# Moving the weight stream from the scalar engine's DMA queue to the sync engine's, with new orders for blocks 1 to 7

## What is computed

```python
xn = _layernorm(x)
x = x + attn(xn) + ffn(xn)

# attn: chunked linear attention with decay, 16 heads of 32, chunks of 128 tokens
h = _rmsnorm(xn, qkv_norm_w); q, k, v = h @ ternary(qkv_w).T
scores = einsum('bhtd,bhsd,hts->bhts', qi, ki, mask)
intra  = einsum('bhts,bhsd->bhtd', scores, vi)
cross  = einsum('bhtd,ht,bhde->bhte', qi, lam_t, S)
S      = lam_T * S + einsum('bhtd,ht,bhte->bhde', ki, lam_rev, vi)
out = _rmsnorm(_rmsnorm(intra + cross, norm_w), proj_norm_w) @ ternary(proj_w).T

# ffn: 512 -> 2048 -> 512
gated = silu(xn @ w_gate.T) * (xn @ w_up.T)
y = gated @ w_down.T
```

## Time and profile before

| | |
|---|---|
| median of 3 runs | 1535.77 us (1535.44 to 1554.81) |
| profiled execution, whole | 1534.2 us |
| its span, first to last instruction | 1532.4 us |
| TensorE busy (PE) | 1339.8 us, 87% |
| its weight loads (PEld, beside PE) | 903.7 us, 59% |
| VectorE busy (DVE) | 1088.7 us, 71% |
| ScalarE busy (ACT) | 648.5 us, 42% |
| GpSimd busy (POOL) | 294.3 us, 19% |
| queue q1 (SP) | 125.09 MB, 35.2% of the 16 engines' span |
| queue q10 (ScalarE) | 88.10 MB, 18.5% |
| mean granted TensorE clock | 0.959 of full |

### The profile page before, as it was taken

One profiled execution on the slowest core, in us unless ns is written; L12 is line 12 of the kernel. 1 busy time (PEld: TensorE's weight loads), 2 busy tenths in 40 slices (PEclk: granted clock), 3 DMA queues, 4 the chain that ended last, 5 costly groups with the idle time before them and its releaser, 6 DMA issues.

```text
span 1532.4 us, 26734 instructions
## 1 busy us (share of the span) xinstructions
PE 1339.8 (87%) x10060; PEld 903.7 (59%) x10060; DVE 1088.7 (71%) x2118; ACT 648.5 (42%) x1275; POOL 294.3 (19%) x296
## 2 busy tenths in 40 slices
PE   5899999988689988889987899888987889878899
PEld 3465545543376664666756676576755767557675
DVE  6989966977556786567865689476893658946576
ACT  7955424655233352334524335243442433424342
POOL 5400001455111211112111122011220112201111
PEclk9999999999889999999999999899998999989999
DMA  7232342477955349553594435944468543595342
GB/s 295 93 101 90 77 124 87 161 232 233 220 139 132 121 128 167 138 141 111 146 181 127 136 107 146 199 131 108 128 162 160 140 91 127 148 163 147 87 132 54
DMA packets 242558, 214.89 MB, mean 140 GB/s; under 512 B 147456, under 2 KB 212992, under 8 KB 240768
## 3 DMA queue, kind: packets, MB, share of 16 engines
q1 hardware_dynamic: 228320, 125.09, 35.2%
q10 hardware_dynamic: 14112, 88.10, 18.5%
HBM read 130.82 MB, written 23.07 MB: 100 GB/s over the span
## 4 chain that ended last, share of the span: by engine, by line
PE 55%; DVE 18%; issue 9%; DMA 8%; SPq 5%; ACT 3%; POOL 2%; ACTq 0%; DVEq 0%; POOLq 0%
PE bank L679 30%; PE bank L811 22%; DMA k_stack<-k_parts 4%; SPq L1234 3%; DVE stage L995 2%; DMA q_stack<-q_parts 2%; PE bank L721 2%; DVE arena L1109 2%; DVE wide L1661 1%; DMA wide<-up_t 1%; SPq L1335 1%; DVE sm_lo L995 1%; DVE xin L1132 1%; DVE sm L1037 1%; SPq L1236 1%
## 5 line engine op out<-in xcount | busy, mean ns | idle before, releaser
L811 PE MATMUL bank<-wide 128*128 128x256 f16 x4032 | 498.2, 281 | 38.3 <-issue 38.1
L811 PEld LDWEIGHTS bank<-wide 128*128 128x128 f16 x4032 | 402.8, 101 | 100.6 <-issue 40.9
L679 PE MATMUL bank<-wd_hi,arena 128*128 128x512 f16 x1024 | 326.3, 385 | 17.1 <-DVE arena L1109 14.5
L1204 POOL TENSOR_TENSOR wide<-wide 128x512 f32<-128x512 f32 x96 | 125.9, 1314 | 823.8 <-ACT wide L958 823.8
L679 PE MATMUL bank<-wd_lo,arena 128*128 128x512 f16 x512 | 197.1, 385 | 0.0
L679 PE MATMUL bank<-xt,wide 128*128 128x512 f16 x768 | 178.1, 387 | 6.7 <-ACT sg L972 3.3
L679 PEld LDWEIGHTS bank<-wd_hi,arena 128*128 128x128 f16 x1024 | 101.4, 99 | 138.3 <-DVE arena L1109 18.8
L1109 DVE SCALAR_TENSOR_TENSOR arena<-bank,small,arena 128x512 f32<-128x512 f32 x160 | 119.4, 746 | 41.3 <-PE bank L679 31.1
L1037 DVE TENSOR_TENSOR sm<-bank,mask 128x512 f32<-128x512 f32 x128 | 87.6, 684 | 71.9 <-PE bank L721 71.6
L679 PE MATMUL bank<-ht,wq 128*128 128x256 f16 x1024 | 127.6, 274 | 7.2 <-DVE arena L1109 3.5
L872 ACT ACTIVATE sm_hi<-sm 128x512 f16<-128x512 f32 x128 | 80.0, 625 | 127.0 <-DVE sm L1037 126.9
(11 more groups left out here) (215 smaller groups left out, 1928.4 us busy)
## 6 DMA issues: line engine op xcount, KB each, us to landing
wide<-made ACTq DMA_DIRECT2D x96, 896.0 KB, 5.6
made<-wide SPq DMA_DIRECT2D x16, 896.0 KB, 5.4
k_stack<-k_parts SPq DMA_DIRECT2D x192, 64.0 KB, 2.2
q_stack<-q_parts SPq DMA_DIRECT2D x192, 64.0 KB, 2.3
arena<-x SPq DMA_DIRECT2D x8, 1024.0 KB, 5.9
out<-arena SPq DMA_DIRECT2D x32, 256.0 KB, 10.4
xin<-x SPq DMA_DIRECT2D x30, 256.0 KB, 4.7
stage<-up_t SPq DMA_DIRECT2D x4, 1024.0 KB, 5.4
```

The source lines that it names most:

```text
L679: last = e.matmul(dst, a, b, start=start and n == 0, stop=stop and n == len(lhs) - 1)
L811: last = e.matmul(dst, tile_weights(h, n // 2, w, k), tile_x(n % 2, b, k), start=start and (k, n) == (0, 0), stop=(k, n) == (1, 2), skip_g ...
L1204: e.tensor_tensor(up[h % 2], up[h % 2], gt[h % 3], ALU.mult).then_inc(po["GT"].sem, 1)
```

## The change

ScalarE's list loses item `LW` (16 a steady block, 4 in block 1). SP's list gets the same items, with the same waits and the same transfer: the stream now runs in q1, first in, first out with the fills of the stacks, the loads, the stores and the transposes. The lists of blocks 1 to 7 are written anew on all engines; each holds the same items as before. In block 1 the two transposes of `xs` become an item `MC` of their own. Block 0's lists are as before.

```diff
-    return it[0] in ("ST", "XN", "TX", "TT", "XC", "TH", "XT") or it[0] == "LW" and it[1] >= HT
+    return it[0] in ("ST", "XN", "TX", "TT", "XC", "TH", "XT", "MC") or it[0] == "LW" and it[1] >= HT
...
-        elif kind == "LW":
-            h = it[1]
-            if is_plain(blk):
-                e.wait_ge(st_b[BUILD_SLOT[h - HT]], 16 * turn(h - HT))
-                e.wait_ge(pe["U"].sem, pe["U"].at(blk, 12 if h < HT + 2 else HT))
-            else:
-                e.wait_ge(pe["P3"].sem, pe["P3"].at(blk, h - RING + 1))
-            e.dma_start(ring[h % RING], made[h % HT, :, :]).then_inc(ld_w[h % RING].sem, 16)
...
-                    elif kind == "LW" and is_plain(blk) and n == HT + 2:
+                    elif kind == "LW":
+                        if is_plain(blk):
+                            e.wait_ge(st_b[BUILD_SLOT[n - HT]], 16 * turn(n - HT))
+                            e.wait_ge(pe["U"].sem, pe["U"].at(blk, 12 if n < HT + 2 else HT))
+                        else:
+                            e.wait_ge(pe["P3"].sem, pe["P3"].at(blk, n - RING + 1))
+                        e.dma_start(ring[n % RING], made[n % HT, :, :]).then_inc(ld_w[n % RING].sem, 16)
+                    elif kind == "MC":
                         for m in range(2):
                             e.wait_ge(st_b[m], 16 * BUILD_SLOT.count(m))
                         for p in range(2):
```

Of the steady list of SP, two lines:

```diff
-        ('K', 0), ('Q', 0), ('V', 0), ('KT', 0), ('K', 1), ('Q', 1), ('KT', 1), ('K', 2), ('Q', 2), ('KT', 2), ('K', 3),
+        ('K', 0), ('Q', 0), ('V', 0), ('KT', 0), ('LW', 4), ('Q', 1), ('K', 1), ('KT', 1), ('LW', 5), ('LW', 6), ('LW', 7),
```

More of the change, by code:

```diff
@@ L166 @@
     "PE": [
[3 rows of a table removed]
[3 rows of a table added]
         ('SC', 2, 0), ('U', 3), ('KV', 2), ('O', 2, 0), ('SC', 2, 1), ('Q', 3), ('K', 3), ('G', 4), ('U', 4), ('OX', 2, 0),
[10 rows of a table removed]
[10 rows of a table added]
     ],
     "ACT": [
[14 rows of a table removed]
[14 rows of a table added]
     ],
     "DVE": [
[18 rows of a table removed]
[18 rows of a table added]
     ],
     "POOL": [
-        ('BA', 0), ('BA', 1), ('NR', 0), ('BA', 2), ('BA', 3), ('ST', 0), ('BA', 4), ('BA', 5), ('BA', 6), ('BA', 7),
-        ('BA', 8), ('BA', 9), ('TT', 0), ('BA', 10), ('BA', 11), ('BA', 12), ('BA', 13), ('NR', 1), ('BA', 14), ('BA', 15),
+        ('BA', 0), ('BA', 1), ('NR', 0), ('BA', 2), ('ST', 0), ('BA', 3), ('BA', 4), ('BA', 5), ('BA', 6), ('BA', 7),
+        ('TT', 0), ('BA', 8), ('BA', 9), ('BA', 10), ('BA', 11), ('BA', 12), ('BA', 13), ('NR', 1), ('BA', 14), ('BA', 15),
         ('ST', 1), ('TT', 1),
@@ L234 @@
     "PE": [
[17 rows of a table removed]
[18 rows of a table added]
     ],
     "ACT": [
[17 rows of a table removed]
[15 rows of a table added]
     ],
     "DVE": [
[20 rows of a table removed]
[19 rows of a table added]
     ],
     "POOL": [
-        ('UG', 0), ('UG', 1), ('UG', 2), ('UG', 3), ('UG', 4), ('UG', 5), ('UG', 6), ('UG', 7), ('UG', 8), ('NR', 0),
-        ('ST', 0), ('UG', 9), ('UG', 10), ('TT', 0), ('UG', 11), ('UG', 12), ('UG', 13), ('UG', 14), ('UG', 15), ('NR', 1),
+        ('UG', 0), ('UG', 1), ('UG', 2), ('UG', 3), ('UG', 4), ('UG', 5), ('UG', 6), ('UG', 7), ('NR', 0), ('UG', 8),
+        ('UG', 9), ('UG', 10), ('ST', 0), ('TT', 0), ('UG', 11), ('UG', 12), ('UG', 13), ('UG', 14), ('UG', 15), ('NR', 1),
         ('ST', 1), ('TT', 1),
```

## The result

The changed kernel takes 1383.74 us (median, 1378.71 to 1388.07) against 1543.55 for the kernel before in the same comparison: ratio 0.896, 95% interval 0.888 to 0.904. That is 160 us, more than twice the 73 that were forecast, and 41 us under the low end of the range. Measured once more on another chip the ratio was 0.895 (0.891 to 0.899).

What follows compares the result with a forecast made beforehand. TensorE sets the pace, with 144 us idle in blocks 2 to 7, mostly behind DMAs, and clock 0.95. 39 + 0 + 8 + 40 + 12 - 26 = 73 us off 1534.2 gives 1461, median 1463; range 1425 to 1522.

Steps and rivals of the forecast that it cites:

- waits before `SC`: TensorE waiting for stack fills: 28 us saved at `SC 1 0`, 12 at other steps, 26 charged for the shared queue.
- what the queue adds: Fills behind loads in q1 at steps 2, 4, 5, 6, 7: 26 us lost, about 2 at two places a block.
- starts of blocks 3 to 7: Waits before the first tile work for the second `xs` transpose go whole: 30.0 us.
- passage to block 2: Block 1 to 2: VectorE's later chain and a clean transpose cancel, 0; bounds 5 gained, 10 lost.
- slow matmuls: Matmuls slowed after long waits speed up: 9 us at block starts, 12 after `SC 1 0`.
- Block starts: First tile work, steady blocks: clean second `xs` transpose saves 30 us of waits and 9 of slow matmuls; bounds 30 and 39.
- `KV 0` and `SC 1 0`: Early products and `SC` whose transfers have loads beside them: 8 us and 40 us saved, the latter including slow matmuls.
- The other stack waits: Waits for `k_stack` and `q_stack` fills: a quarter of 47.7 us, 12, saved; bounds 0 and 30.
- the block starts alone: Rival, chance 0.18: only block starts gain, queue losses eat `SC`, `KV` and stack gains; 1497 us.
- Block 1: Block 1 and its passage to block 2: 0 taken; bounds 5 us gained, 10 lost.
- All of it: Rival, chance 0.12: new lists land every fill in time, 130 us less 20 for meeting VectorE; 1426 us.
- the signs named for the forecast: Second `xs` transpose 6 to 9 us, `SC 1 0` wait under 2 us, clock over 0.96, idle near 85 us.

Runs made afterwards that it cites:

- The two loads alone: `LW 18` and `LW 19` moved ahead in ScalarE's list, right behind `TD 15`, queue unchanged, against the kernel before: 1494.81 us, ratio 0.969.
- Alone 41: `LW 4` to `LW 7` of blocks 2 to 7 moved from ScalarE's list to SP's, against the kernel before: 1501.63 us, ratio 0.974.
- the ten loads in question: `LW 8` to `LW 17` of blocks 2 to 7 moved from ScalarE's list to SP's, against the kernel before: 1497.56 us, ratio 0.983.

## Why the prediction was wrong

The direction, the places and the loads as the cause held; the size did not, by a factor of 2.2. The step that failed is the account of the waits before `SC`: 28 and 12 us saved, less 26 for what the queue adds. In the two profiled executions, 146 us apart, it can be told term by term:

| | forecast | measured |
|---|---|---|
| waits before `SC` | 28 + 12 - 26 = 14 | 82.0 - 26.5 = 55.5 |
| starts of blocks 3 to 7 | 30 | 30.0 |
| passage to block 2 | 0 | 3.5 + 8.1 - 11.6 = 0 |
| `KV 0` (`issue` waits on L679) | 8 | 12.3 - 1.0 = 11.3 |
| all other waits of TensorE | none | 53.1 - 42.3 = 10.8 |
| slow matmuls (busy time) | 9 + 12 = 21 | 1339.8 - 1301.0 = 38.8 |
| sum | 73 | 146.4 |

Of the 73 us that the forecast lacks, 41.5 lie in the first row.

**Block starts, 39 us forecast.** Right in place and cause. The two loads alone are worth 47 us (0.969). The clean transpose lands in 6.1 us, as 6.4 had been taken.

**`KV 0` and `SC 1 0`, 48 us forecast.** Alone 41, with 16 more handed to the next block start. About right. `SC 1 0` was to keep a wait of 1 us; it keeps 0.15 to 0.5, and 1.21 in block 6.

**The other stack waits, 12 us forecast, and the queue's cost, -26.** Here the sum failed. Together they stood for -14 us. Moving the ten loads in question gives +26, and the group effect another 11. The reasoning was that a fill in q1 must wait for a whole load ahead of it, up to 5.6 us. The unit price held (3.1 to 4.7 measured). But I charged it at two places a block, though I had just worked out that TensorE has 5.4 to 9 us of work at these places, enough for the fill and about one load. The fills do go out behind loads in flight, and that work covers them: the waits before `SC` in the whole changed kernel are 26.5 us in 33, where the earlier trace rows had 82 and the forecast left 68. Nor did the quarter taken for the other stack waits have a row behind it: with the ten loads moved, 47.7 us became 16.5.

**The queue itself.** The rule quoted from *DMA: Bandwidth & Descriptors* of the Trainium skill, section "Issuing engines are not separate DMA queues", has no place for what weighs most. At nearly the same moments of issue, ScalarE's queue costs 70 us against SP's. The page is right that the transfers interleave; where the trace shows it, it is the interleaving that costs, since a transpose and two loads need 24 us side by side and 11 in a row. The prediction saw 17.0 against 6.4 us in the earlier trace rows and called it the price of what the queue and the loads put in the transpose's way; it had no term for a rate that falls when the two kinds mix. The rival "the block starts alone", which leaned on the same rule, is out.

**Block 1, 0 forecast, 5 gained as a bound.** Measured 11 by ratios, 7 to 10 in the profiles. The passage to block 2 takes about as long as before, as worked out; the gain is inside the block, where the earlier trace rows was my only look.

**The lists.** From all loads on SP under the old lists to the changed kernel is 0.919 to 0.896, 35 us: 11 of it block 1's, the rest in the steady blocks, where `wide<-made` (10.7 us), `KV` and the adds before `PJ` no longer wait. The prediction had no term for it beyond the waits that it listed.

**The clock.** 9 + 12 = 21 us were taken for slow matmuls that go; TensorE's busy time in blocks 2 to 7 fell by 979.9 - 944.6 = 35. I had counted them at the two largest waits only, though shorter ones are followed by some as well: behind the 2.56 us wait of the earlier trace rows pairs of `D`'s matmuls take 0.89 to 1.06 us where such a pair takes 0.59 elsewhere.

**The range.** "All of it" ended at 1426 since it subtracted 20 us for VectorE, which did not become the bound at 75% busy, and held only waits that I had named. With 144 us idle and a clock of 0.95 standing in the earlier trace rows, the low end should have come from the floor: TensorE's work at full clock with a few per cent of waits.

Of the signs named for the forecast, all came true but one: the second transpose landed in 6.1 us, no first tile work waited for it, `SC 1 0` waited under 2 us and the clock was 0.99, but the idle time of blocks 2 to 7 was 37 us, not 85.

## What to carry to other kernels

When a large copy stream and small transposing DMAs run at once, try them in one queue, ordered by hand: here the same transfers at nearly the same moments were 70 us dearer in two queues. Keeping them apart in time within two queues helps as well (47 us for two loads a block); whether that could give all of it was not tried. Price a transfer behind another, place by place, by how much work its consumer has left meanwhile. And when the busiest engine idles 13% in many short waits behind one kind of transfer, let the low end of the range reach close to its busy time.

## What the runs showed of the hardware

In block 4 a DMA transpose of 128x28x128 and two loads of 896 KB take 11 us one behind the other in one queue and 24 us in two queues, and each is slowed: 23.5 us against 9.4, and 12.5 against 5.9. Over all blocks the longest landing of an `xs` transpose is 10.7 us in the changed kernel and 22.3 with the loads in the other queue at nearly the same moments, with the median of the 56 small ones 2.6 and 3.5:

```profile
L1335 SPq DMA_TRANSPOSE stage<-stage x56: 1196/1249/2494, 213.3 to 1347.8; - x56
...
DMA to landing us min/median/max: 2.5/2.6/7.8
```

```profile
L1346 SPq DMA_TRANSPOSE stage<-stage x56: 1196/1274/2090, 213.6 to 1413.6; - x56
...
DMA to landing us min/median/max: 2.5/3.5/11.5
```

Why two queues are slower than one (whether it is the transposing or the small packets, of which the kernel has 147456 under 512 B) was not tried; it would take a copy of small packets in place of the transpose. Nor was it tried to hold the loads in ScalarE's queue until the transposes beside them have landed, which would tell one queue from mere order.
